# A hybrid vision block on one NeuronCore: filler matmuls removed from the neighbourhood attention, and the routed attention's projections moved to other PSUM banks

## The reference, cut to what is computed

```python
x = L0(x)        # layernorm -> 7x7 neighbourhood attention (4 heads of 16, bias table) -> + x -> layernorm -> MLP(GELU)
t = x.reshape(2, 1024, 64)
t = t + L1(ln(t))        # global attention, 8 heads of 64 over 1024 tokens
t = t + routed(ln(t))    # a scan over 33 steps:
def step(h, p):
    op = argmax(h[0, 0, :19])                       # the data choose an operation
    q, k, v = h @ wq[op], h @ wk[op], h @ wv[op]    # h is (8, 512, 64) in the reference's set-up, (2, 1024, 64) here
    y = softmax(q @ k.T / 8) @ v @ wo[op]
    h = where(attn_mask[op], y, h)
    z = relu(h @ w1[op] + b1[op]) @ w2[op] + b2[op]
    h = where(ffn_mask[op], z, h)
```

## Time and profile before

| | us |
|---|---|
| median of 3 runs (580.57 to 582.08) | 580.86 |
| the profiled execution | 581.07 |
| its span, first to last instruction | 579.3 |
| neighbourhood attention | 26 to 130 |
| start of the global attention, PE at 1.2 GHz for some of it | 130 to 155 |
| global attention | 155 to 450 |
| first feed-forward, choices, loads | 450 to 488 |
| routed projections | 488 to 497 |
| routed attention | 497 to 552 |
| second feed-forward, choice, output | 552 to 579 |

### The profile page before, as it was taken

How to read it: one execution, slowest core, us unless ns; L and a number is a source line. 1 busy time by engine, 2 the same in 40 slices (tenths; PEclk the granted TensorE clock), 3 DMA queues, 4 the chain that set the end, 5 groups by cost and what they waited for, 6 DMA issues and landing times.

```text
span 579.3 us, 12657 instructions
## 1 busy us (share of the span) xinstructions
PE 498.3 (86%) x5167; PEld 254.8 (44%) x5168; DVE 391.8 (68%) x724; ACT 293.4 (51%) x440; POOL 56.3 (10%) x108
## 2 busy tenths in 40 slices
PE   6898898875899899999999999999999362699871
PEld 5565665651334354444444444444444121377621
DVE  5875767579766558768866876766743366898562
ACT  2765466651454845455555555456555233655440
POOL 8152143131100000000000000000000000000000
PEclk9999999998799999999999999999999876999975
DMA  4201000000000000000000000000000000000001
GB/s 113 45 2 38 1 2 1 2 20 0 2 1 1 1 1 3 1 19 3 1 2 1 1 3 1 11 2 1 2 1 1 2 2 15 1 1 1 2 0 36
DMA packets 10224, 5.01 MB, mean 9 GB/s; under 512 B 9012, under 2 KB 9271, under 8 KB 10167
## 3 DMA queue, kind: packets, MB, share of 16 engines
q1 hardware_dynamic: 8886, 4.19, 3.2%
q10 hardware_dynamic: 1281, 0.01, 0.1%
HBM read 2.09 MB, written 0.52 MB: 5 GB/s over the span
## 4 chain that ended last, share of the span: by engine, by line
PE 64%; DVE 17%; issue 10%; ACT 5%; POOL 2%; DVEq 0%; SPq 0%; DMA 0%; POOLq 0%; ACTq 0%
PE PS L802 17%; PE PS L778 16%; PE PS L762 5%; DVE most L1580 4%; PE PS L818 3%; PE PS L530 2%; PE PS L502 2%; PE PS L514 2%; PE PS L1018 2%; PE PS L692 2%; DVE sbias L1626 2%; PE PS L705 2%; PE PS L603 1%; ACT PT L1215 1%; PE PS L719 1%
## 5 line engine op out<-in xcount | busy, mean ns | idle before, releaser
L1580 DVE TENSOR_REDUCE most<-PS 128x2 f32<-128x1024 f32 x128 | 156.1, 1222 | 81.8 <-PE PS L762 80.9
L1215 ACT ACTIVATE PT<-PS 128x1024 f32<-128x1024 f32 x128 | 124.5, 1021 | 117.5 <-PE PS L778 117.5
L778 PE MATMUL PS<-qS,aS 64*64 64x512 f16 x1024 | 123.4, 380 | 1.8 <-ACT PT L1215 1.6
L778 PE MATMUL PS<-qS,kS 64*64 64x512 f16 x1024 | 123.0, 380 | 0.0
L802 PE MATMUL PS<-PT,V 128*64 128x512 f32 x512 | 121.8, 596 | 0.0
L778 PEld LDWEIGHTS PS<-qS,kS 64*64 64x64 f16 x1024 | 58.1, 108 | 25.2 <-issue 1.0
L778 PEld LDWEIGHTS PS<-qS,aS 64*64 64x64 f16 x1024 | 58.1, 108 | 25.1 <-ACT PT L1215 4.6
L762 PE MATMUL PS<-aS,qS 64*64 64x512 f16 x256 | 51.9, 399 | 11.2 <-DVE most L1580 10.8
L802 PEld LDWEIGHTS PS<-PT,V 128*64 128x64 f32 x512 | 34.0, 137 | 46.4 <-issue 42.3
L1172 ACT ACTIVATE prob<-sbias,negm 128x320 f32<-128x320 f32 (+1 forms) x64 | 34.3, 539 | 36.4 <-DVE negm L1626 35.7
L762 PE MATMUL PS<-kS,qS 64*64 64x512 f16 x256 | 51.9, 399 | 0.0
(11 more groups left out here) (200 smaller groups left out, 714.6 us busy)
## 6 DMA issues: line engine op xcount, KB each, us to landing
xall<-in_x_dram SPq DMA_DIRECT2D x2, 256.0 KB, 4.4
qS<-kS SPq DMA_DIRECT2D x4, 128.0 KB, 2.6
q0M<-kS SPq DMA_DIRECT2D x4, 128.0 KB, 2.4
kS<-aS SPq DMA_DIRECT2D x4, 128.0 KB, 2.3
out_dram<-x SPq DMA_DIRECT2D x4, 128.0 KB, 2.1
w<-in_L_attn_Wq_dram SPq DMA_DIRECT2D x2, 128.0 KB, 2.5
w<-in_L_attn_Wk_dram SPq DMA_DIRECT2D x2, 128.0 KB, 2.7
w<-in_L_attn_Wv_dram SPq DMA_DIRECT2D x2, 128.0 KB, 2.7
```

The costliest lines, as they stand in the source:

```text
L778: mm = pe.matmul(PS[h0:h0 + C, score_banks(t) + lane, :], input_of(lane, k_part)[:, k0 + h0:k0 + h0 + C], qS[C * lane:C * lane + C, q_part ...
L1215: act.activation(PT[:, g % 2, :, phase, :], PS[:, b0:b0 + 2, :], ACT.Exp).then_inc(c1["exped"], 1)
L1580: dve.tensor_reduce(most[:, g % 2, u // 2, u % 2, :], PS[:, try_bank(a):try_bank(a) + 2, :], AX.X, ALU.max, negate=True)\
```

## The change

Two edits that have no instruction in common.

First, `keep_busy` and its 64 matmuls are gone. Second, in `attend` the eight k and q pieces lie in banks 4 to 7 instead of 0 to 3. The v pieces are no longer in the loop: they are made behind score 0, in banks 4 and 5, and each is copied by ScalarE alone in one instruction of 512 columns. Score 0 waits for five drained pieces (k of both lanes and the first q piece), score 1 for all eight; the v copies are waited for behind score 3, ahead of the first transposes, which reuse banks 4 and 5. The counts `N_HIGH` (14, ScalarE's) and `N_SPLIT` (12, VectorE's) part accordingly.

```diff
             def nat_turn(u):
...
-                keep_busy(bank)
                 for n, (_, k, _) in enumerate(key_chunks(u // NH0 % NT)):
...
+            pieces_drained(5)
             score(0)
+            project_values(0)
+            project_values(1)
+            pieces_drained(8)
             score(1)
             for i in range(n + LAG_Y + 3):
                 if i + 2 < n:
                     score(i + 2)
+                if i == 1:
+                    values_drained()
...
-                for n in range(len(ROUTED)):
+                for n in range(8):
...
-                    bank = PS[:, n % 4, :]
...
+                        m = pe.matmul(PS[:, 4 + n % 4, :], w, hS[:, t0:t0 + BLK], start=(part == 0), stop=(part == 1))
                     m.then_inc(routed_filled, 1)
-                pe.wait_ge(routed_split, bp + N_SPLIT)
-                pe.sem_inc(gate, 1)
+
+                def project_values(blk):
+
+                    pe.wait_ge(routed_split, bp + 4 + 5 + blk)
+                    pe.sem_inc(gate, 1)
+                    bank = PS[:, 4 + blk, :]
...
+                def pieces_drained(n):
+
+                    pe.wait_ge(routed_split, bp + 4 + n)
...
                 if what == "v":
-                    half = QT // 2
-                    ins = act.activation(V[:, blk * QT:blk * QT + half, :],
-                                         bank[:, 0:half * P].rearrange("p (t c) -> p t c", t=half), ACT.Copy)
+                    ins = act.activation(V[:, blk * QT:(blk + 1) * QT, :],
+                                         bank.rearrange("p (t c) -> p t c", t=QT), ACT.Copy)
...
-                if what == "v":
-                    half = QT // 2
-                    ins = dve.tensor_copy(V[:, blk * QT + half:(blk + 1) * QT, :],
-                                          bank[:, half * P:].rearrange("p (t c) -> p t c", t=half))
-                elif what == "k":
+                if what == "k":
```

More of the change, by code:

```diff
@@ L101 @@
 YH = 4
-FILL = 256
 LAG_PV, LAG_OUT, LAG_Y, LAG_YD = 3, 11, 11, 12
@@ L673, in _ @@
             pe.wait_ge(w_loaded, W_LOADS)
-            def keep_busy(bank):
-                filler = ident[:, :].bitcast(F16)
-                pe.matmul(bank[:, 0:FILL], filler[:, 0:P], filler[:, 0:FILL], start=True, stop=True)
             def nat_score(u):
@@ L977, in attend, with values_drained @@
                     what, lane, blk = ROUTED[n]
-                    bank = PS[:, n % 4, :]
-                    if what == "v":
-                        for j in range(QT):
-                            for lane in range(2):
-                                t0 = lane * TOK + (blk * QT + j) * P
-                                for part in range(2):
-                                    m = pe.matmul(bank[:, j * P + C * lane:j * P + C * lane + C], hS[:, t0:t0 + P],
-                                                  wsS[:, part, 2, 0, :], start=(part == 0), stop=(part == 1))
-                    else:
-                        t0 = lane * TOK + blk * BLK
-                        for part in range(2):
-                            w = wsS[:, part, "kq".index(what)].rearrange("p a c -> p (a c)")
-                            m = pe.matmul(bank, w, hS[:, t0:t0 + BLK], start=(part == 0), stop=(part == 1))
-                    m.then_inc(routed_filled, 1)
-                pe.wait_ge(routed_split, bp + N_SPLIT)
-                pe.sem_inc(gate, 1)
+                    t0 = lane * TOK + blk * BLK
+                    for part in range(2):
+                        w = wsS[:, part, "kq".index(what)].rearrange("p a c -> p (a c)")
+                        m = pe.matmul(PS[:, 4 + n % 4, :], w, hS[:, t0:t0 + BLK], start=(part == 0), stop=(part == 1))
+                    m.then_inc(routed_filled, 1)
+                def project_values(blk):
+                    pe.wait_ge(routed_split, bp + 4 + 5 + blk)
+                    pe.sem_inc(gate, 1)
+                    bank = PS[:, 4 + blk, :]
+                    for j in range(QT):
+                        for lane in range(2):
+                            t0 = lane * TOK + (blk * QT + j) * P
+                            for part in range(2):
+                                m = pe.matmul(bank[:, j * P + C * lane:j * P + C * lane + C], hS[:, t0:t0 + P],
+                                              wsS[:, part, 2, 0, :], start=(part == 0), stop=(part == 1))
+                    m.then_inc(routed_filled, 1)
+                def pieces_drained(n):
+                    pe.wait_ge(routed_split, bp + 4 + n)
+                    pe.sem_inc(gate, 1)
+                def values_drained():
+                    pe.wait_ge(routed_high, bh + N_HIGH)
+                    pe.sem_inc(gate, 1)
                 def y_of(g, lane):
@@ L1262, in attend @@
                     act.wait_ge(routed_filled, base(len(ROUTED)) + (n + 1))
-                    high_part(piece, PS[:, n % 4, :], (1.0, C ** -0.5), routed_high)
+                    high_part(piece, PS[:, 4 + n % 4, :], (1.0, C ** -0.5), routed_high)
                 act_attention(act, c2, base, 2)
@@ L1848, in attend @@
                 base = lambda k: dve.snap(na * k)
-                by, bp = base(N2["y"]), base(N_SPLIT)
-                low_state(routed_high, routed_split, bp, range(2), 2)
+                by, bh = base(N2["y"]), base(N_HIGH)
+                low_state(routed_high, routed_split, bh, range(2), 2)
                 keys_left(attend_keys, base(NKEYS))
@@ L1853, in attend @@
                 for n, rows in enumerate((slice(0, C), slice(C, P))):
-                    dve.wait_ge(routed_high, bp + (3 + n))
+                    dve.wait_ge(routed_high, bh + (3 + n))
                     dve.tensor_tensor(wsS[rows, 1], twice, wsS[0:C, 0], ALU.subtract).then_inc(routed_split, 1)
-                for n, piece in enumerate(ROUTED):
-                    dve.wait_ge(routed_high, bp + (4 + n + 1))
-                    low_part(piece, PS[:, n % 4, :], (1.0, C ** -0.5), routed_split)
+                for n, piece in enumerate(ROUTED[:8]):
+                    dve.wait_ge(routed_high, bh + (4 + n + 1))
+                    low_part(piece, PS[:, 4 + n % 4, :], (1.0, C ** -0.5), routed_split)
                 def y_out(g, lane):
```

8 lines of the change are left out of this document (4 added, 4 removed).

## The result

The changed kernel takes **576.35 us** in the median of 5 runs (575.43 to 578.55), against 580.86 us (579.80 to 582.08, 5 runs) for the kernel before on the same chip: ratio 0.9922, with a 95% interval of 0.9903 to 0.9941. That is 4.5 us less; 4.1 us were forecast.

What follows compares the result with a forecast made beforehand. No engine owns the neighbourhood attention, where TensorE and VectorE take turns; at the routed start VectorE, TensorE and VectorE run in series. 581.07 - 2.3 (filler) - 1.8 (routed start) = 577.0 us; range 575.2 to 582.0 us, 8 times in 10.

Steps and rivals of the forecast that it cites:

- The filler's price: Neighbourhood attention: fillers cost only on the chain of waits, 3.5 us at most; two thirds, 2.3 us, would come back.
- What is late next: Neighbourhood loop without fillers: VectorE is late next; its wait for transposes shrinks from 15.6 us by about 2 us.
- The cover: Neighbourhood loop: fillers may help the clock rise at about 31.2 us; losing them costs nothing, or up to 7.8 us.
- Both rivals of a late rise: Neighbourhood loop: without fillers the clock rises late, 580.6 us (chance 0.23), or very late, about 584 us (chance 0.16).
- the late rise: Neighbourhood loop: the clock rises at about 38 us, costing 3.6 us more, 580.6 us in all; chance 0.23.
- A fall within the loop: Neighbourhood loop: the prediction is wrong if the clock falls there; small chance, priced like the first loss of the clock.
- very late rise: Neighbourhood loop: clock low until the fp32 projections at 42.55 us, 6.3 to 7.8 us more, about 584 us; chance 0.16.
- The routed start: Start of routed attention: earlier score 0 and no v copies on VectorE bring the first maximum 1.86 us earlier; 1.8 us taken.
- The sum: Whole kernel: 2.3 us from the filler and 1.8 us from the routed start, giving 577.0 us; chance 0.47.
- The later stages: Stages behind the edits: only move earlier; meeting clock changes may differ by execution, 1 us added to each side.

Runs made afterwards that it cites:

- e6: The kernel before with only the 29 fillers that lie on its chain of waits; 581.60 us, ratio 1.0005 to the kernel before.
- e7: The kernel before with only the 35 fillers that are not on its chain of waits; 579.39 us, ratio 0.9954 to the kernel before.
- e8: The changed kernel with half of each v copy given back to VectorE, ahead of the first maximum, early score kept; 578.29 us, ratio 0.9951 to the kernel before.
- e1: The kernel before without its 64 fillers and nothing else changed; 578.98 us, ratio 0.9964 to the kernel before.
- e2: The changed kernel with its fillers put back, leaving only the routed edit; 578.57 us, ratio 0.9960 to the kernel before.
- e3: The kernel before with the filler called twice in each unit; 584.04 us, ratio 1.0055 to the kernel before.
- e4: The changed kernel with 62 fillers ahead of the waits of 13 scores in the neighbourhood loop; 576.02 us, ratio 0.9913 to the kernel before.
- e5: The changed kernel with fillers ahead of the waits of six of the middle stage's first scores; 575.16 us, ratio 0.9897 to the kernel before.
- e12: e11 without the 12 fillers behind the last state turn, and with 8 moved from the feed-forward's start to the attention's end; 572.53 us, ratio 0.9853.
- e9: The changed kernel with score 0 put behind both v pieces, all drains and ScalarE's v copies; 579.36 us, ratio 0.9961 to the kernel before.
- e11: The changed kernel with the fillers of e4, e5 and e10 together; 573.39 us, ratio 0.9859 to the kernel before.
- e10: The changed kernel with fillers behind the last two state turns and at the starts of routed attention and feed-forwards; 573.94 us, ratio 0.9878 to the kernel before.

## Why the prediction was right, point by point

**The filler's price.** It was the step on the chain, not the duration: between units 16 and 36 14 such steps, 1.54 us, and 1.41 us came back. e6 and e7 show that the chain had named the right ones. Up to the bias of unit 36 the chain has two fillers at 0.21 us and 22 at 0.11, together 2.84 us, and 2.49 us came back, 88%. (With the five later ones that is 29 in all. The prediction counted some 29 beside the two at the lower clock; its sum of 3.5 us, read from the chain, stands.) Of the five later ones (0.72 us) some 0.2 us did, read from e8, whose clock did not fall there: its lead over the kernel before, 0.77 us of which it has at unit 0, grows from 3.25 us at the bias of unit 44 to 3.45 at that of unit 63. In all that is three quarters of 3.5 us; the two thirds of the prediction were chosen by judgement between none and all, and that they came out near is partly luck, for the split is another one: nearly all where TensorE leads without a break, little where it leads for a step or two. By the times the 2.3 us became 2.2 in e1, whose loop also had a late rise and a fall of the clock, and 2.7 in e7 by its ratio.

**What is late next.** VectorE, as said: its wait for transposes fell by the 2.0 us that were named, and TensorE's wait for it grew by as much.

**The cover.** Both rivals of a late rise fell. The clock rose between 29.4 and 32.3 us in all 14 profiles, with 0 to 128 fillers in the loop and in no order of their number:

```
kernel                      rise, us
before (64 fillers)         31.2
after (0)                   30.9
e1 (0)                      32.3
e2 (64)                     32.1
e3 (128)                    29.4
e4 (0 ahead of unit 8)      29.4
e6 (29), e7 (35)            30.4, 29.7
e5, e8 to e12 (0 there)     30.0 to 31.4
```

TensorE is busy for 3.45 of the 4 us from 27 to 31 us without fillers, in scores and transposes. 0.39 of chance stood on these rivals; the argument against them, that at half speed the real work closes the gaps by itself, should have had more weight. The price of the late rise was too high besides: 4.05 us at half speed do the work of 2.0, so a rise at 38 us would have cost some 2 us and not 3.6; in e6 the 3.4 us from 33.8 to 37.2 us cost 1.56. The Trainium skill, TensorE: Matmul & The Clock Gate, Part 4 (PE-mode transpose), by which transposes don't count as busy in the way that matmuls do, spoke for the late rise. The trace doesn't bear out what I drew from it: transposes shortened from 0.64 to 0.38 us behind a stretch of scores and transposes alone. It is no refutation of the rule itself, since the scores between them may have been enough. Nor were the fillers over a third of what that rule would have counted: by their steps before, the three took 0.64 us beside some 2.0 us of scores (0.93, 0.53 and 0.53), about a quarter of the whole.

**A fall within the loop.** The prediction said it would be wrong if the clock fell there; it did, in the profiled execution, and the forecast held all the same, since the fall cost about 1 us (0.8 lost from unit 44 to 63, where e8 gains 0.2) and not the 6 to 8 us of a very late rise. So that sign of being wrong was set too sharp. Such a fall needs no missing filler: e2 has all 64 and the same work up to there as the kernel before, and fell at 90.1 us. Windows of e2:

```profile
87.00:90.00 3.00, 1.06 (x10) 0.71 (x8) 2.86 (x8) 0.74 (x2) 0.00 (x0) 1.00 0.00 0
90.00:93.00 3.00, 3.00 (x33) 1.63 (x31) 2.54 (x9) 1.73 (x5) 2.43 (x3) 0.52 0.00 0
```

The kernel before has the same 1.06 us in the first of these stretches and no fall behind it. Whether fillers make such a fall rarer can't be told from one profile of each kernel; that stays open.

**The routed start.** The changed kernel reaches its pieces 0.52 us earlier than the kernel before, so 0.52 us are added to its times here. Score 0 at 494.10 (forecast about 494.0), first maximum at 495.66 (495.76), first exponential at 496.91 (497.02). The v copies took 0.54 us each (0.59) and left 0.2 us ahead of the exponential (0.1). The two maxima took 2.52 us instead of 2.35, so the second was held by 0.17 us (0.15). The gain up to the last exponential is 1.79 us (1.8). e8 and e9 show that both parts are needed, which is what the series of VectorE, TensorE and VectorE meant. By the medians the edit gives somewhat more, 2.6 us in e2; the trace has 1.8 of it in its place, and the rest is within the interval of 1.5 to 3.2 us.

**The sum.** Forecast 2.3 + 1.8 = 4.1 us, measured 4.5; by their places in the traces the two terms are 2.7 (2.5 up to unit 36 and 0.2 behind it) and 1.8. The later stages were given 1 us to each side for meeting changes of the clock; in the profiled execution they took 1.6 us at 137 to 154 us and gave 0.45 back by the first matmul of the pieces.

## What to carry to other kernels

A filler matmul costs its step on the chain of waits where TensorE leads and nothing where TensorE waits; so read the chain with the order of the program beside it, and never put a filler ahead of a step that is due. Fillers in the waits of stages where the clock falls are worth a try: in many places at once (e11, e12) they took the kernel clearly below the changed one, in one stage alone (e4, e5) the times can't tell them from nothing. When engines hand over in series at the start of a stage, look for the two conditions of the first step together: freeing one engine gave 0.3 us here, the early score 0.8, and both 1.8.

## What the runs showed of the hardware

The granted clock differs between executions of the same kernel, and with it the time. In e1 the run with a mean clock of 0.954 that was shortest took 577.49 us, and the longest at 0.945 took 580.50; in e6 it was 580.14 us at 0.954 and 585.00 at 0.942. Over the 32 runs of the kernel before with e6 to e9 time and mean clock have a correlation of -0.79. So part of the spread within a kernel goes with the clock.

Short falls of the clock between 87 and 95 us are in the profiles of the changed kernel, e1, e2, e6, e7 and e9, and not in those of before, e3, e4, e5, e8 and e10 to e12. They cost 0.7 to 1.2 us each, as the start of unit 48 against unit 43 shows.

A longer low stretch costs less than its length, since there TensorE waits much of the time: 17.1 us low instead of 10.3 us, around 145 us, cost 1.6 us. Nor does the cost grow evenly: from maximum 8 to maximum 16 the kernels with 13.6 us low there (e4, e6, e7, e9) take as long as the kernel before with its 10.3, to within 0.01 us, e3 with 10.3 us too takes 0.7 us less, and those without a low stretch there (e11, e12) 2.1 us less.
